# Attention maxima into guard rows: a product with the identity against a number-by-number DMA through device memory

## The reference, cut to what matters

```
Q = einsum('btd,hkd->bthk', x, W_Q) + b_Q      (16 heads of 64; K and V likewise)
scores = einsum('bqhk,bshk->bhqs', Q, K) / sqrt(64)
attn = softmax(scores, axis=-1)
out_h = einsum('bhqs,bshk->bqhk', attn, V)
x = x + einsum('bqhk,hdk->bqd', out_h, W_O) + b_O
```

## Time and profile before

| what | value |
|---|---|
| three timed runs | 1110.34, 1111.82, 1113.67 us; median 1111.82 |
| the profiled execution, own time | 1110.69 us |
| its span in the profile | 1109.4 us |
| mean granted TensorE clock | 0.989 |
| busy: PE / DVE / ACT / POOL | 96% / 78% / 57% / 69% |
| attention | from the start to about 690 us |

### The profile page before, as it was taken

One profiled execution on the slowest core, in us unless ns is written; L12 is line 12 of the kernel. 1 busy time (PEld: TensorE's weight loads), 2 busy tenths in 40 slices (PEclk: granted clock), 3 DMA queues, 4 the chain that ended last, 5 costly groups with the idle time before them and its releaser, 6 DMA issues.

```text
span 1109.4 us, 18601 instructions
## 1 busy us (share of the span) xinstructions
PE 1062.7 (96%) x6804; PEld 657.3 (59%) x6804; DVE 865.3 (78%) x1246; ACT 628.6 (57%) x930; POOL 765.5 (69%) x400
## 2 busy tenths in 40 slices
PE   8999999999999999999999999979789997999998
PEld 4555665665665665665665656967344443446786
DVE  6878987787786785776986748336999999997987
ACT  5454554554553554643553545448885776657653
POOL 5688889788788797777899840330888899794200
PEclk9999999999999999999999999989899999999999
DMA  7000110110110110110110353574655454440000
GB/s 215 1 21 21 40 29 13 39 34 8 39 35 7 39 41 7 34 36 5 45 31 20 116 163 104 147 242 135 210 188 171 142 162 135 133 153 19 10 10 20
DMA packets 63882, 83.72 MB, mean 75 GB/s; under 512 B 24368, under 2 KB 42768, under 8 KB 63792
## 3 DMA queue, kind: packets, MB, share of 16 engines
q1 hardware_dynamic: 60784, 79.45, 23.4%
q0 software_dynamic: 1024, 2.10, 0.6%
q10 hardware_dynamic: 1984, 0.98, 0.3%
HBM read 75.98 MB, written 6.28 MB: 74 GB/s over the span
## 4 chain that ended last, share of the span: by engine, by line
PE 76%; issue 8%; DVE 7%; POOL 5%; DMA 2%; ACT 2%; SPq 0%; ACTq 0%; POOLq 0%; DVEq 0%
PE psum L684 20%; PE psum L640 15%; PE psum L670 6%; PE psum L658 4%; PE psum L975 4%; PE psum L1069 4%; PE psum L710 3%; PE psum L1052 3%; POOL hc L2322 3%; PE psum L769 3%; PE psum L725 2%; DVE mx L1683 2%; PE psum L703 2%; DVE psum L1993 2%; PE psum L749 1%
## 5 line engine op out<-in xcount | busy, mean ns | idle before, releaser
L2234 POOL TENSOR_TENSOR psums<-psums,prob 128x1024 f32<-128x1024 f32 x180 | 430.8, 2393 | 26.1 <-POOL psums L2234 0.5
L1683 DVE TENSOR_REDUCE mx<-psum 128x2 f32<-128x1024 f32 x256 | 299.7, 1217 | 100.4 <-PE psum L670 100.1
L1190 ACT ACTIVATE prob<-psum 128x1024 f32<-128x1024 f32 x228 | 232.7, 1027 | 59.6 <-PE psum L658 38.9
L684 PE MATMUL psum<-prob,V 128*64 128x512 f32 x1024 | 238.7, 597 | 0.0
L2322 POOL TENSOR_TENSOR hc<-hs,cc 128x1024 f32<-128x1024 f32 x64 | 151.4, 2366 | 19.7 <-DVE hs L2000 17.0
L2000 DVE TENSOR_TENSOR_SCAN hs<-dA,psum 128x1024 f32<-128x1024 f32 x64 | 146.3, 2286 | 2.2
L684 PEld LDWEIGHTS psum<-prob,V 128*64 128x64 f32 x1024 | 67.7, 137 | 106.7 <-issue 105.0
L975 PE MATMUL psum<-hc,ident 128*128 128x512 f32 x256 | 124.5, 610 | 2.9 <-DVE slot_rows_h L2008 1.5
L2234 POOL TENSOR_TENSOR psums<-prob 128x1024 f32<-128x1024 f32 x30 | 72.1, 2404 | 78.9 <-ACT prob L1190 78.9
L1209 ACT COPY oraw<-psum 128x512 f32<-128x512 f32 x32 | 18.8, 587 | 178.1 <-PE psum L684 178.1
L670 PE MATMUL psum<-k_hi,q_hi 64*128 64x512 f32 x512 | 107.1, 410 | 1.8 <-DVE mx L1683 1.3
(11 more groups left out here) (322 smaller groups left out, 1789.1 us busy)
## 6 DMA issues: line engine op xcount, KB each, us to landing
cc<-C_rows SPq DMA_DIRECT2D x64, 512.0 KB, 3.7
slot_rows_h<-guard_rows SPq DMA_DIRECT2D x56, 256.0 KB, 3.3
kq_wts<-in_e_rows SPq DMA_DIRECT2D x14, 578.0 KB, 4.8
e_wts<-in_e_rows SPq DMA_DIRECT2D x10, 578.0 KB, 4.1
e_w<-in_e_rows SPq DMA_DIRECT2D x6, 578.0 KB, 5.4
slots_in<-e_zero SPq DMA_DIRECT2D x2, 960.0 KB, 7.2
inv<-sum_rows SPq DMA_DIRECT2D x120, 1.0 KB, 2.1
slots_out<-e_y SPq DMA_DIRECT2D x30, 64.0 KB, 2.4
```

Source lines behind the costliest of these rows:

```text
L684: ins = pe.matmul(A.O[HALF[s], :], A.V[pair % 2][:, j, s * DH:(s + 1) * DH], A.prob[unit(pair, c, j) % NPB][:, s * CH:(s + 1) * CH], start ...
L1190: act.activation(A.prob[n % NPB][:, :], slots.bank("score", pair, c, j).rearrange("p s n -> p (s n)"), ACT.Exp, scale=float(DH) ** -0.5).t ...
L1683: dve.tensor_reduce(K.A.mx[:, :, t, c], slots.bank("max", pair, t, c), AXX, ALU.max).then_inc(*slots.inc("max", pair, t, c))
L2234: pool.tensor_tensor(total[:, :], (K.A.prob[(n - 1) % NPB] if j == 1 else total)[:, :], K.A.prob[n % NPB][:, :], ALU.add).then_inc(*K.psum ...
```

## The change

For pairs 2 to 15, `dve_cols` writes the negated maxima into a small tile of their own (`A.negated`, 128 partitions by 2 heads by 8) instead of `A.nmx`. SP gets a new step `store_guard` straight behind `cols`: one DMA that writes these 2048 numbers to `A.guard_rows` in device memory in the order head, tile, partition, each number by itself. In the place of `row` and `rowed`, SP gets a step `set_guard`: it waits until the store has landed and issues two DMAs from `A.guard_rows` to the guard rows, 4 KB each into one partition. `pe_row`, `dve_row` and the four DMAs out of `A.mrow` are gone for these pairs; pairs 0 and 1 keep them. `spread_guard` is as before, but for the semaphore level.

```
@@ phase
     if c == NC - 1:
-        order.append(("cols", nxt))
+        order += [("cols", nxt), ("store_guard", nxt)]
     order.append(("shift", pair, c, NT - 1))
...
-        order += pv[j:j + 1] + beside[j] * (j < NT - 1) + [("row", nxt), ("rowed", nxt)] * (c == NC - 1 and j == 3)
+        order += pv[j:j + 1] + beside[j] * (j < NT - 1) + [("set_guard", nxt)] * (c == NC - 1 and j == 3)
         order += [("spread_guard", nxt, 0)] * (c == NC - 1 and j == 4 and nxt < LAST)
...
+def guard_stored_level(pair):
+    return 32 + 16 * (pair - 1)
@@ dve_cols
     dve.wait_ge(*K.slots.empty("max", pair, ts.stop - 1, NC - 1))
+    if pair > 1:
+        if pair > 2:
+            dve.wait_ge(A.guard_stored, guard_stored_level(pair - 1))
+        dve.tensor_reduce(A.negated[:, :, :], A.mx[:, :, :, :], AXX, ALU.max, negate=True).then_inc(*K.nmx_done.inc(pair))
+        return
@@ dve_row
-    if k[0] > 1:
-        dve.wait_ge(K.A.guard_stored, 32 * (k[0] - 1))
@@ sp_row
-    if pair > 1:
-        sp.wait_ge(*K.slots.full.at("score", pair - 2, NC - 1, NT - 1))
     for s in range(2):
         sp.dma_start(A.guard[q][s * LO:s * LO + 1, :].rearrange("o (t k) -> o t k", t=NT)[:, ts, :].bitcast(F32),
                      A.mrow[s * LO + ts.start:s * LO + ts.stop, :].bitcast(F32)).then_inc(A.guard_set[q], 16)
-    if 0 < pair < LAST:
-        if pair > 1:
-            sp.wait_ge(A.guard_spread, guard_spread_level(pair - 1, 1))
+    if pair == 1:
         for s in range(2):
             sp.dma_start(A.guard_rows[s], A.mrow[s * LO:s * LO + NT, :].bitcast(F32)).then_inc(A.guard_stored, 16)
+def sp_store_guard(K, sp, pair):
+    A = K.A
+    sp.wait_ge(*K.nmx_done.at(pair))
+    sp.wait_ge(A.guard_spread, guard_spread_level(pair - 1, 1))
+    if pair > 2:
+        sp.wait_ge(A.guard_set[(pair - 1) % 2], guard_level(pair - 1))
+    sp.dma_start(A.guard_rows.rearrange("s t k -> k s t"), A.negated.bitcast(F32), allow_slow_non_contiguous=True).then_inc(A.guard_stored, 16)
+def sp_set_guard(K, sp, pair):
+    A, q = K.A, pair % 2
+    sp.wait_ge(A.guard_stored, guard_stored_level(pair))
+    sp.wait_ge(*K.slots.full.at("score", pair - 2, NC - 1, NT - 1))
+    for s in range(2):
+        sp.dma_start(A.guard[q][s * LO:s * LO + 1, :].bitcast(F32), A.guard_rows[s:s + 1].rearrange("o t k -> o (t k)")).then_inc(A.guard_set[q], 16)
@@ sp_spread_guard
-    sp.wait_ge(A.guard_stored, 32 * pair)
+    sp.wait_ge(A.guard_stored, guard_stored_level(pair))
```

More of the change, by code:

```diff
@@ L2509, in sp_added @@
     sp.dma_start(K.out.rearrange("(t p) d -> p t d", p=P)[:, at, :], K.x[:, at, :]).then_inc(K.stored, 16)
-SP_STEPS = {"row": sp_row, "spread_guard": sp_spread_guard, "sums": sp_sums, "rows": sp_rows, "fetch": sp_fetch, "yrow": sp_yrow, "loads": sp_loads, "e1_load": sp_load_experts,
+SP_STEPS = {"row": sp_row, "spread_guard": sp_spread_guard, "store_guard": sp_store_guard, "set_guard": sp_set_guard, "sums": sp_sums, "rows": sp_rows, "fetch": sp_fetch, "yrow": sp_yrow, "loads": sp_loads, "e1_load": sp_load_experts,
             "xpj_out": sp_store_C, "unit": sp_unit, "added": sp_added}
@@ L2651, in two_layer_program @@
             A.mx, A.nmx, A.mrow = sba("mx", [P, 2, NT, NC]), sba("nmx", [P, P]), sba("mrow", [P, P], F32R)
+            A.negated = sba("negated", [P, 2, NT], F32R)[:, :, :]
             A.inv, A.sum_rows = sba("inv", [P, 2 * NT]), [sba(f"sum_rows{c}", [P, P, 2]) for c in range(NC)]
```

## The result

The changed kernel takes 1151.9 us (median of six runs, 1148.6 to 1157.8) against 1111.1 for the kernel before in the same series: a ratio of 1.037, 95% interval 1.035 to 1.039, or 41 us more. The forecast was 1108.7 and the range ended at 1131. It went the way of the first rival. The profiled execution took 1157.8 us with a span of 1156.4. It is the slowest of the six, so it lies 47 us above the profiled one of before, where the medians differ by 41.

The account below looks back on a forecast made before the run. It took PE to bound the kernel, so 14 removed products of 0.22 us give 3.1 us, other terms nothing: 1111.8 - 3.1 = 1108.7 us. The range went from 1106.3 to 1131 us.

Parts of the forecast that it names:

- the range: Whole kernel's time: from 1106.3 us to 1131, the store at 10.3 us; 0.13 left out above.
- the first rival: At PE's guard product (L658): store misses its deadline and PE stalls, from 8.3 us on; 1131 to 1174 us; chance 0.28.
- What bounds the kernel, and the product's worth: PE in the attention: PE bounds it; the product with the identity holds it 0.22 us, 14 times, 3.1 us.
- the sum: Whole kernel: only PE's removed product counts, 3.1 us off the 1111.8 median, giving 1108.7.
- The deadline: Negated maxima to PE's next guard product: 11.1 us, less a 2.8 us load leg, leaves the store 8.3.
- How long the store takes: SP's store of 2048 single numbers to device memory, issue to landing: taken at 7 us.
- The upper bound of 33.6 us: Store's landing: 16 times a small DMA's 2.1 us, if all of that went with the number of packets.
- Its price rule: PE's stall at the guard product: store's excess over 8.3 us in eleven pairs, over about 10 in three.
- "Traffic behind the store": SP's queue: four sums DMAs may land only behind the store, at 317 to 318; DVE's reciprocal at 322.73 still served.

Follow-up runs that it names:

- no_rows: Kernel before without negating, product, copy and guard DMAs for pairs 2 to 15, nothing in their place: ratio 0.996, 4.6 us less.
- idle_store: Kernel before plus, per pair, a store of 2048 single numbers to device memory that nothing waits for until the program's end: ratio 1.011, 12 us more.
- wide_store: Changed kernel with each stored number on its own 64 bytes of device memory, guard rows loaded from there with a stride: ratio 1.089.
- sorted_by_act: Changed kernel, maxima sent by DMA as 32-byte pieces into the guard tile, ACT sorting them into guard rows, without device memory ahead: 0.997 of kernel before.

## Why the prediction was wrong

- *What bounds the kernel, and the product's worth.* Right. L734 goes from 68 records to 12, and no_rows gives 4.6 us (3.1 to 6.0) for the 3.1 of the sum, with the negation, the copy and four DMAs gone too.
- *The deadline.* Right in kind, and a little too tight: the load leg was put at 2.8 us and took 1.9, so the store had some 9.2 us, not 8.3.
- *How long the store takes.* This is the step that failed. It was put at 7 us by the nearest row, the zeroing of `slots_in` with 1920 packets of 512 bytes, and by the DMA engines' 9 ns per small packet. It takes 11.4 us in the kernel (10.8 to 12.4). The engines' part was right, they are through in about 2 us; but the landing is not the engines' busy time. No row of the kernel before has single numbers written side by side into device memory, and that is what costs. The upper bound of 33.6 us did hold it; the value taken inside the bounds came from rows that lack the property that matters.
- *Rival 1* named the place, the sign and the point of decision, and had 0.28. Its price rule (excess over 8.3 us in eleven pairs, over 10 in three) gives +35 us at 11.4 us, near the measured +41. That is partly luck, for two errors offset each other: it would have PE stand 38 us, where it stood 28 with the shorter load leg, and it has no low clock, worth 17 to 18. Its reason, a price for each packet, is refuted: 128 numbers took 6.8 to 9.4 us and 2048 10.4.
- *A cost not in the sum.* The prediction counted a stall at its length. The low clock behind the stalls was some 18 of the 41 us. The kernel before had shown full clock throughout the attention, so no row asked for it, but the earlier trace rows did show that this engine's clock can fall.
- *"Traffic behind the store" on SP's queue.* It was said that the sums' DMAs might report late, and that this would cost nothing. It costs nothing for them (in the last pair DVE waited 9.3 us for them, but their result was wanted only 17 us later), but the same holding back cost the old guard DMAs 12 us in idle_store. In the changed kernel nothing but the loads stands behind it with a deadline.
- *The range* ended at a store of 10.3 us and left out 0.13 above. The store was 11.4, and the clock came on top: 28 us of waits cost some 45 (28 + 17), 1.6 times their length.

What stays open: why single numbers side by side land late in device memory. The distance between starts matters (8 bytes apart still cost 7.8 to 9.0 us, 16 bytes 5.0 to 5.1), the count hardly does, and 8-byte writes side by side are quick, so the size of each write may be what decides; no run varies it alone. Open too: why single numbers are slow to write into one partition of SBUF.

## What to carry to other kernels

A DMA that turns a 4-byte matrix number by number into device memory is priced by how close together the single numbers land, not by its bytes or packets. Here it helped to put them 16 bytes or more apart, or to write two numbers (8 bytes) in one packet; but reading the spread-out numbers back into one partition then took 9.8 us (wide_store). What won was to keep the numbers that lie together in one packet and let an idle engine put them in order (sorted_by_act). A slow landing also holds back the semaphores of the DMAs behind it, so a store that nobody waits for can still cost. Where PE is the bound, a stall can cost more than its length, for the clock may drop behind it: here 1.6 times, over stalls of 0.3 to 5.1 us.

## What the runs showed of the hardware

- 2048 single numbers to neighbouring places in device memory land in 10.4 to 12.4 us, 128 of them in 6.8 to 9.4, 2048 lone ones in 4.2 to 5.0, 1024 pairs of numbers side by side in 4.4 to 4.6. The DMA engines are done after 2 us in the first case as well.
- A small DMA behind such a store reports after 10.5 us in place of 1.9.
- 1024 single numbers into one partition of SBUF take 7.7 us, the same as 128 pieces of 32 bytes 1.9, and into 128 partitions 2.1.
- A matmul whose moving operand has a stride of 8 numbers holds PE for 0.41 us in place of 0.23.
- In or behind eight of the 14 stalls (1.9 to 5.1 us) the granted clock of PE was at its lower level for 3.4 us, twice for 6.8; with six (0.3 to 1.4 us, and one of 2.3) it was not, nor anywhere in the attention with PE kept at work through the same waits.
- A copy of 1024 numbers on one partition with a stride takes 2.1 us on ACT and 1.3 to 3.2 on DVE.
